# A decoder layer on one Trainium2 core: the second bank of turned probabilities copied by ScalarE

## What is computed

```
scores = q @ k.T / 8 + mask            # 128 x 120
attn   = softmax(scores)               # exp(scores - max), times 1 / sum
ctx    = attn @ v                      # 128 x 64
```

## Time and profile before

| | |
|---|---|
| median of 3 runs | 1701.09 us (1700.48 to 1701.42) |
| the profiled execution, its own time | 1701.68 us |
| span in its trace | 1699.9 us |
| granted TensorE clock, mean | 0.917 of full |
| busy: PE, DVE, POOL, ACT | 1362.3, 1107.3, 852.5, 806.5 us |

### The profile page before, as it was taken

One profiled execution on the slowest core, in us unless ns is written; L12 is line 12 of the kernel. 1 busy time (PEld: TensorE's weight loads), 2 busy tenths in 40 slices (PEclk: granted clock), 3 DMA queues, 4 the chain that ended last, 5 costly groups with the idle time before them and its releaser, 6 DMA issues.

```text
span 1699.9 us, 34078 instructions
## 1 busy us (share of the span) xinstructions
PE 1362.3 (80%) x11168; PEld 1107.9 (65%) x11168; DVE 1107.3 (65%) x2851; ACT 806.5 (47%) x3111; POOL 852.5 (50%) x1012
## 2 busy tenths in 40 slices
PE   2878787889898887989889888889879888886250
PEld 1667666777677766777667766767667676765240
DVE  3566766676767776677767777677757777665233
ACT  3645454555556454555446454455536454452020
POOL 5343426443555457454755447463665537453535
PEclk9999998999999998999989999999989998997575
DMA  6000000111222211221211202222212212222551
GB/s 197 8 7 8 7 7 22 50 55 57 63 75 60 72 37 57 73 70 54 71 59 58 86 29 75 68 62 68 63 42 83 71 41 71 65 62 81 145 158 52
DMA packets 142895, 105.77 MB, mean 62 GB/s; under 512 B 12352, under 2 KB 137856, under 8 KB 142720
## 3 DMA queue, kind: packets, MB, share of 16 engines
q1 hardware_dynamic: 134528, 86.80, 17.6%
q0 software_dynamic: 8192, 16.79, 3.4%
HBM read 69.99 MB, written 33.55 MB: 61 GB/s over the span
## 4 chain that ended last, share of the span: by engine, by line
PE 36%; DVE 19%; POOL 15%; ACT 15%; issue 11%; SPq 2%; DMA 2%; DVEq 0%; ACTq 0%; POOLq 0%
ACT pr L884 11%; DVE nm L1165 5%; PE sE L532 4%; POOL sorted_x L1566 4%; PE t L391 3%; PE ma L391 3%; DVE pT L1176 3%; POOL pr L1538 2%; POOL gat L1578 2%; POOL rs L1545 2%; PE pvb L573 2%; PE t L395 2%; DVE ys L1336 2%; PE t L396 2%; PE t L397 2%
## 5 line engine op out<-in xcount | busy, mean ns | idle before, releaser
L1538 POOL TENSOR_TENSOR pr<-pr,ri 128x480 f32<-128x480 f32 x256 | 252.3, 994 | 430.2 <-DVE ri L1180 429.1
L884 ACT ACTIVATE pr<-sE,nm 128x120 f32<-128x120 f32 x512 | 178.0, 360 | 405.8 <-DVE nm L1165 405.6
L564 PE MATMUL pvb<-pT,vv 120*64 120x128 f32 x2048 | 146.7, 288 | 69.7 <-DVE pT L1176 68.9
L564 PEld LDWEIGHTS pvb<-pT,vv 120*64 120x64 f32 x2048 | 115.9, 142 | 100.0 <-DVE pT L1176 91.2
L884 ACT ACTIVATE pr<-sO,nm 128x120 f32<-128x120 f32 x512 | 179.4, 383 | 0.0
L532 PEld LDWEIGHTS sE<-kT,qT 64*128 64x128 f32 x1024 | 134.8, 202 | 58.1 <-issue 58.1
L1176 DVE COPY pT<-t 120x512 f32<-120x512 f32 x256 | 165.2, 684 | 5.7 <-PE t L391 4.3
L532 PE MATMUL sE<-kT,qT 64*128 64x120 f32 x1024 | 159.4, 300 | 0.0
L532 PE MATMUL sO<-kT,qT 64*128 64x120 f32 x1024 | 159.4, 300 | 0.0
L1578 POOL DMA_INDIRECT gat<-sorted_y,slot x128 | 135.7, 1060 | 32.6 <-issue 30.1
L1566 POOL DMA_INDIRECT sorted_x<-x,slot x128 | 128.3, 1002 | 47.0 <-issue 35.4
(11 more groups left out here) (326 smaller groups left out, 3479.9 us busy)
## 6 DMA issues: line engine op xcount, KB each, us to landing
wq<-in_w_e SPq DMA_DIRECT2D x232, 128.0 KB, 2.0
sorted_y<-yq SPq DMA_DIRECT2D x64, 256.0 KB
xq<-sorted_x SPq DMA_DIRECT2D x58, 256.0 KB, 2.8
xt<-in_x SPq DMA_DIRECT2D x16, 256.0 KB, 3.0
sorted_x<-yq SPq DMA_DIRECT2D x16, 256.0 KB, 4.1
out_y<-y SPq DMA_DIRECT2D x64, 64.0 KB, 1.6
cT<-in_ctxT SPq DMA_DIRECT2D x16, 240.0 KB, 3.1
sorted_x<-x,slot POOLq DMA_INDIRECT x128
```

What stands on the lines that cost most here:

```text
L564: ins = mm(pvb[r * DK:(r + 1) * DK, (k // 2) * T:(k // 2 + 1) * T], vv[:, q, h * DK:(h + 1) * DK], pT[:, 4 * r + k // 2, :], start=True, s ...
L884: ins = f(pr[:, p % RING, r, i, :], score_banks[r][:, i * S:(i + 1) * S], ACT.Exp, bias=nm[:, p % 2, r, i:i + 1], accum_out=rsum[:, p % 2, ...
L1538: GP.tensor_tensor(pr[:, p % RING, r, :, :], pr[:, p % RING, r, :, :], ri[:, p % 2, r, :, :].to_broadcast([P, 4, S]), ALU.mult).then_inc(s ...
```

## The change

ScalarE gets a `b_probs_T` of its own: it copies bank t1 (the odd heads) into columns 4 to 7 of pT as the first thing in slots 2 to 9, ahead of the exponentials of that slot. VectorE's `b_probs_T` keeps only the copy of bank t0. The semaphore is split in two, probsT0_sb (VectorE) and probsT1_sb (ScalarE), 8 each per group; `b_pv` waits for both, and the turns wait each for its own. ScalarE has the same wait for pv of the pair before that VectorE has.

```diff
-    "probsT": 16, "probsT_sb": 16, ...
+    "probsT": 16, "probsT0_sb": 8, "probsT1_sb": 8, ...
@@ TensorE, proj_free
-                        pe.wait_ge(sem["probsT_sb"], upto("probsT_sb", b - 1, 14 + n - 4))
+                        pe.wait_ge(sem[f"probsT{n - 4}_sb"], whole(f"probsT{n - 4}_sb", b - 1))
@@ TensorE, b_probs_T
-                        pe.wait_ge(sem["probsT_sb"], upto("probsT_sb", b, 2 * p - 2 + r))
+                        pe.wait_ge(sem[f"probsT{r}_sb"], upto(f"probsT{r}_sb", b, p - 1))
@@ TensorE, b_pv
-                pe.wait_ge(sem["probsT_sb"], upto("probsT_sb", b, 2 * p + 1))
+                for r in range(2):
+                    pe.wait_ge(sem[f"probsT{r}_sb"], upto(f"probsT{r}_sb", b, p))
@@ TensorE, d_T and d_up
-                    pe.wait_ge(sem["probsT_sb"], whole("probsT_sb", G - 1))
+                    pe.wait_ge(sem["probsT1_sb"], whole("probsT1_sb", G - 1))
@@ ScalarE
+            def b_probs_T(b, p):
+                if p:
+                    act.wait_ge(sem["pv"], upto("pv", b, p - 1))
+                elif later(b):
+                    act.wait_ge(sem["pv"], whole("pv", b - 1))
+                act.wait_ge(sem["probsT"], upto("probsT", b, 2 * p + 1))
+                f(pT[:, 4:8, :], seqs(t1[0:S, :]), ACT.Copy).then_inc(sem["probsT1_sb"], 1)
@@ ScalarE, body
                 for s in range(PAIRS + LAG):
+                    if B and s >= LAG:
+                        b_probs_T(b, s - LAG)
                     if B and 0 < s < PAIRS:
                         b_probs(b, s, 0)
@@ VectorE, b_probs_T
-                for k in range(2):
-                    dve.wait_ge(sem["probsT"], upto("probsT", b, 2 * p + k))
-                    V.tensor_copy(pT[:, 4 * k:4 * k + 4, :], seqs((t0, t1)[k][0:S, :])).then_inc(sem["probsT_sb"], 1)
+                dve.wait_ge(sem["probsT"], upto("probsT", b, 2 * p))
+                V.tensor_copy(pT[:, 0:4, :], seqs(t0[0:S, :])).then_inc(sem["probsT0_sb"], 1)
```

More of the change, by code:

```diff
@@ L70 @@
     "ctx_hi": 1, "ctx_split": 1, "proj": 24, "proj_act": 12, "proj_dve": 12, "scores": 16, "negmax": 16, "probs": 16,
-    "probsT": 16, "probsT_sb": 16, "rinv": 16, "normal": 16, "pv": 8, "headsT_sb": 8,
+    "probsT": 16, "probsT0_sb": 8, "probsT1_sb": 8, "rinv": 16, "normal": 16, "pv": 8, "headsT_sb": 8,
     "wo": 4, "attn_sum": 4, "ln2_stats": 4, "ln2_mv": 4, "ln2_eps": 4, "ln2_rstd": 4, "ln2_out": 4,
```

## The result

The changed kernel takes **1663.53 us** (median of 4 runs, 1661.98 to 1665.68) against 1700.78 for the kernel before on the same chip: ratio 0.9782, 95% interval 0.9765 to 0.9799, so 37 us faster. I had forecast 1674 with a range of 1657 to 1692. The direction is right; the gain is 37 us instead of 27. A part of the difference has causes that the prediction had priced at nothing or given a small chance; where another 5 or 6 us of it arise, single executions don't show.

The account below looks back on a forecast made before the run. VectorE and ScalarE take turns, with VectorE's pT copies ahead of the maxima on the path. 45 slots x 0.60 = 27.0 us, ScalarE's copy and waits 0: 1701.7 - 27.0 = 1674.7, less 0.6 for the median, 1674; range 1657 to 1692.

Parts of the forecast that it names:

- What bounds the kernel: VectorE's pair of pT copies ahead of the maxima is on the path; ScalarE waits 405.6 us for those maxima.
- Part 1: VectorE loses 128 copies of 0.60 us; 45 slots on the path pay, 27.0 us; slot 4 keeps both gains.
- Rival (b): In slots 3 to 5 TensorE becomes the bound; only slots 2 and 6 pay, 10 us: 1691; chance 0.15.
- Slot 7 waits for the scores: In plain groups, wherever a mixer runs beside it, slot 7's maximum waits for TensorE's scores, as at 953.81.
- More first maxima that wait for scores than 69: Sign in the changed profile: of VectorE's 128 first maxima, more than 69 wait for TensorE's scores.
- Rival (a): In slot 6 shorter waits keep TensorE's clock up; 9 groups save 1.64 us more each, 15 us: 1659; chance 0.20.
- behind pv a second idle, for the scan, remains: Slot 6, argument against the clock staying up: TensorE still idles after pv, and such waits throttle the clock; no size.
- The scatter groups: Five slots 2, plus 2 and 3 slots of b = 2 and 4, pay 0.60 us each, 6.0 us.
- From slot 3 on POOL sets the pace: Scatter groups: VectorE's norm waits 1.38 us for POOL's rs; 11 slots in b = 6 to 14 not counted.
- Rival (c): Clock falls a second time at the wait for pT, slots 4 and 5; 15 groups, +13 us: 1714; chance 0.05.
- The ends: First group b = 0 adds 3 slots, 1.8 us; last group b = 15 has 5 slots, 3.0 us.
- Parts 2 and 3: ScalarE's 128 copies, 0.604 us each, hidden in its idle; second wait of b_pv and split semaphore: taken as nothing.

Follow-up runs that it names:

- Experiment 1: Changed kernel, VectorE given an unused maximum over bank t0 ahead of its one copy in slots 2 to 9; 1698.97 us, ratio 0.9993.
- Experiment 2: Changed kernel, ScalarE copying bank t1 in slots 3 to 6 only, VectorE doing both copies in the other slots; 1676.27 us, ratio 0.9856.
- Experiment 4: Kernel before, 14 products of the identity on TensorE in slot 6 of every group, ahead of pv and its wait for pT; 1692.17 us, ratio 0.9949.
- experiment 12: Changed kernel, TensorE's waits in even groups from b = 6 filled with 9, 15, 7 and 10 identity products; 1657.93 us, ratio 0.9694.
- experiment 6: Changed kernel, TensorE's output product of slot 3 put ahead of the mixer's turn that waits for POOL's xn; 1662.39 us, ratio 0.9782.
- experiment 3: Changed kernel, ScalarE copying bank t1 only in groups with odd b, VectorE doing both copies in the others; 1673.88 us, ratio 0.9845.
- experiment 8: Changed kernel, ScalarE copying the first bank too, ahead of the second, VectorE copying none; 1641.62 us, ratio 0.9660.
- experiment 7: Kernel before, VectorE still doing both copies but the one of bank t1 behind the slot's two maxima; 1716.3 us, ratio 1.0103.
- experiment 11: Changed kernel, VectorE's one copy put behind the slot's two maxima; 1691.52 us, ratio 0.9933.
- experiment 5: Changed kernel, TensorE's waits in even groups from b = 2 filled with 18, 26, 14 and 12 identity products; 1674.21 us, ratio 0.9847.

## Why the prediction was right in direction and short in size

**What bounds the kernel: right.** The pair of copies ahead of the maxima was the path. Experiment 1 shows it without a remainder: with 0.61 us of other work in the same place 0.07% is left of the gain of 2.2%.

**The sum, piece by piece.** The prediction had 16.2 us in the plain groups 1 to 13, 1.8 in b = 0, 6.0 in the scatter groups and 3.0 in b = 15. The two traces show 22.8, 3.7, 5.3 and, up to POOL's last product in b = 15, 2.7; another 3.5 stand behind that product, and 0.4 are lost at the start. Of the surplus of 10.5 us, 6.6 are thus in the plain groups and have a cause below. Of the pieces at the two ends the traces of single executions give no cause.

**Part 1, the 0.60 us and the slots: right in the plain groups.** Four slots in b = 9 give 0.6 each; in slot 4 both gains were kept, so the margin of 0.4 us to the scores held. Experiment 2 puts slots 3 to 6 at 24.5 us; of the 27.0, nearly all but the 3 for slots 2 belonged to them. Rival (b), that the scores swallow the gain, fell with that.

**"Slot 7 waits for the scores": the first step that failed.** I had read it in a trace in which the clock was down in slot 7. With the clock up the scores are there first and VectorE decides again, 5.9 us instead of 6.5 (experiment 2). The wait was a consequence of the clock and I treated it as a property of the slot. "More first maxima that wait for scores than 69" was wrong too. They are fewer, 61: five of slot 7 no longer wait for this reason, in slot 3 it is one instead of six (scatter groups, and b = 1), and in slot 4 nine instead of seven:

```profile
DVE nm L1176 <- PE sO L532: 53.3, 61, 2.9
```

**Rival (a), the clock, at 0.20: the second.** It came in every plain group from b = 5 on, though not in b = 1 and 3 (0.61 and 0.76 in slot 7). The prediction itself had named a clock of 1.00 in slot 7 as the sign that (a) holds and the forecast doesn't; so the time fell into the range, and near the forecast, with the forecast's mechanism and a part of (a)'s together. Its mechanism was as written and its price nearly so: 1.9 us in the step less 0.6 from VectorE is 1.3, where I had 1.64, and it came in five of the nine groups that I had counted. What failed is the argument against it, "behind pv a second idle, for the scan, remains". I had worked out that the first wait halves, and not what that does to the second. The sum of the two went from 2.80 to 2.54 us only, but in two pieces of 1.12 and 1.42. Experiment 4 shows that this clock is worth something in the step itself, 7.8 to 6.7 us, and that the fall then comes later in the group and takes it back; so (a) paid its full price only in b = 9, 11 and 13, while b = 5 and 7 got 3.3 and 2.8 us in all. The Trainium skill, "TensorE: Matmul & The Clock Gate", A second HAM failure mode: psum-queue depth-cycling, says of another kernel that short idles between its groups of products, frequent enough, made the clock go down and up again, and that this cost throughput. Experiments 4 and 12 agree: where the waits were filled, the clock stayed at 1.00. Which length or place of idle makes it fall the runs don't settle. In the changed kernel slot 6 has waits of 1.10 and 1.42 us in b = 5 and of 1.12 and 1.42 in b = 9, and the clock fell behind the last maximum of the one and not of the other; the wait of 2.84 us in slot 3 left it up in b = 6 and 8 and not in b = 10, 12 and 14.

**The scatter groups: right in sum, wrong in kind.** I took 5 slots 2 at 0.6 and 5 slots in b = 2 and 4, 6 us; they gave 5.3. But it is +1.7, +3.9, +1.6, +0.6 and then -0.8, -0.8 and -1.0. "From slot 3 on POOL sets the pace" was half the mechanism. POOL's xn is earlier by 0.6 us only, so of the 1.5 us that maximum 3 had gained 0.6 are left in b = 8: that half was right. TensorE waits longer for it, and in b = 10, 12 and 14 its clock falls and the queued output product runs at the low level, 1.6 us more; that price is the clock's, and experiment 12 removes it. Moving the output product (experiment 6) shortens this slot by 3 us and is given back elsewhere. Rival (c) had this mechanism, a new fall of the clock. It had the wrong place (the wait for pT instead of the one for xn), and it came in three scatter groups, and behind the last maximum of b = 5 and 7, so it cost a few us and not 40.

**The ends.** b = 0 gave 3.7 us (1.8 predicted). In the trace of the kernel before one step of b = 0, from maximum 3 to 4, took 9.1 us at a clock of 0.64; experiments 3 and 4 leave that step's code as it was and took 6.9 there at 1.00. So 2.2 of the 3.7 us may be a difference between two executions. b = 15 with what follows gave 6.2 (3.0 predicted). Of these, 2.7 us lie before POOL's last product with the reciprocals; from its start the changed kernel takes 160.9 us and the one before 164.4. Experiment 4, whose code is the one before's there, takes 162.3, and the others 161.2 to 166.9 (the longest in experiment 12, on the chip where all was slower). So those 3.5 us may be one too. The medians tie all of the 37 us to VectorE's time (experiment 1); in which groups the last 5 or 6 of them arise is open.

**Parts 2 and 3 at nothing: right.** ScalarE's copy takes 0.60 us as in the earlier trace rows:

```profile
L881 ACT ACTIVATE pT<-t x128: 597/598/659, 75.8 to 1507.0; 120x512 f32<-120x512 f32 x128
```

It and the second wait of pv cost nothing that can be measured (experiment 1). The rule that gives simple work to VectorE (the Trainium skill, "ScalarE: Activation LUTs", Rules for kernel authors) names relu, max, min, add and mul, and a speed for bf16; this f32 copy out of PSUM goes the other way, 0.598 us on ScalarE against 0.681 on VectorE, and with both copies on ScalarE the kernel is quickest (experiment 8).

**Open**: whether experiments 8 and 12 add up was not tried; why the clock falls in two plain groups of experiment 6 and not in the changed kernel is only described, not explained; and the median of experiment 7 is 14 us above the one execution whose trace there is. The group lengths come from one execution of each kernel, and single groups with the same code differ by up to 2 us between executions.

## What to carry to other kernels

In a loop of slots, ask for each operation ahead of the critical one both what it delays and what it releases. Putting a copy behind the critical operation costs what it gains, or more, if a product that the same engine later waits for hangs on it and nothing else fills TensorE until then (experiments 7 and 11, in their first groups above all); give it to an engine that is idle at that time, even the whole of it (experiment 8). When one wait gets shorter, work out the next waits of TensorE in its written order, sum and pieces, because the granted clock can turn on them: a slot read as bound by the scores at a clock of 0.6 can be bound by VectorE at 1.00. Products that only fill a wait pay where they are sized from a measured row and fit into the wait (experiment 12), and cost more than the clock gives where they don't (experiment 5).

## What the runs showed of the hardware that I had not expected

- ScalarE's copies of 120x512 f32 out of PSUM follow each other at 0.49 us (875.70 and 876.19, experiment 8), VectorE's at 0.60 (920.54 to the maximum at 921.14, experiment 1).
- A 128x128 f32 product of the identity costs TensorE about 0.24 us at the high clock: it stands as two records, and 18 records (9 products) took 2.17 us, 28 (14 products) 3.39. I had sized them at half of that in experiment 4.
- With the same 11168 records TensorE was 27 us less busy in the changed kernel, and 32 in experiment 8. What differs in its rows is the clock: the eight turns take 1.04 us or 1.92, the output product 1.95 or 3.31.
- A fall of the clock that was gone at one idle came back at another of the same group in several cases: from slot 7 to 7 to 21 us after the last maximum (experiment 4, and b = 5 and 7 of the changed kernel), from slots 2 and 3 (0.62, 0.91) to slot 3 (0.85) and to the stretch 14 to 21 us behind the last maximum (0.60 instead of 0.79) in b = 10 of the changed kernel. In b = 9, 11 and 13 it did not come back.
- The same wait does not always bring the same clock: 2.84 us for xn in slot 3 left it at 1.00 in b = 6 and 8 of the changed kernel and at 0.85 in b = 10, 12 and 14.
